# A three-layer cross-interaction tower: layer 0 from squares of pair sums, states spread over partitions by 0/1 matmuls, and a fully unrolled program

## What is computed

```python
e = stack([tbl_f[ids[:, f]] for f in range(32)], axis=1)      # (1024, 32, 16)
xk = x0 = e
for W in (W0, W1, W2):                                         # (32, 32, 64), (32, 64, 64), (32, 64, 64)
    xk = relu(einsum('bmd,bhd,mhk->bkd', x0, xk, W))
    outs.append(sum(xk, axis=2))
h = concatenate([concatenate(outs, axis=1), dense_ctx], axis=1)
h = maximum(h @ W_top1 + b_top1, 0); h = maximum(h @ W_top2 + b_top2, 0)
y = h @ W_top3
```

## Time and profile before

| what | value |
|---|---|
| runs | 786.91 us median of 3 (784.26 to 787.66) |
| profiled execution, first to last instruction (span) | 775.5 us |
| what the median has beside that span | 11.4 us |
| busy: TensorE, DVE, ACT, POOL | 593.1, 595.6, 408.5, 576.2 us |
| mean granted TensorE clock | 0.921 of full speed |

### The profile page before, as it was taken

How to read it: one execution, slowest core, us unless ns; L and a number is a source line. 1 busy time by engine, 2 the same in 40 slices (tenths; PEclk the granted TensorE clock), 3 DMA queues, 4 the chain that set the end, 5 groups by cost and what they waited for, 6 DMA issues and landing times.

```text
span 775.5 us, 8340 instructions
## 1 busy us (share of the span) xinstructions
PE 593.1 (76%) x2532; PEld 189.3 (24%) x2532; DVE 595.6 (77%) x325; ACT 408.5 (53%) x724; POOL 576.2 (74%) x340
## 2 busy tenths in 40 slices
PE   0256563998289978969499959769599959799998
PEld 0133111322023222213123212213132212222243
DVE  0143459999399969879799958799899969899910
ACT  0123480867238673746357745727367726657522
POOL 6775679698868889898868888898978887626400
PEclk9968795999779998989799999999899989999999
DMA  3799989794979789797979698897979697990000
GB/s 88 160 195 210 204 180 202 156 206 91 204 147 208 151 170 203 152 205 151 204 150 205 118 201 173 182 199 155 205 152 204 136 207 151 203 197 8 7 8 0
DMA packets 56099, 123.07 MB, mean 159 GB/s; under 512 B 16177, under 2 KB 25265, under 8 KB 56082
## 3 DMA queue, kind: packets, MB, share of 16 engines
q1 hardware_dynamic: 47890, 120.75, 76.8%
q0 software_dynamic: 8192, 2.11, 3.0%
HBM read 117.84 MB, written 4.20 MB: 157 GB/s over the span
## 4 chain that ended last, share of the span: by engine, by line
POOL 27%; DVE 18%; issue 16%; DMA 15%; PE 14%; ACT 5%; SPq 4%; POOLq 0%; DVEq 0%; ACTq 0%
DVE prod L455 16%; POOL gath L377 16%; POOL prod_pool L416 11%; PE acc L662 10%; DMA x<-x_scratch 8%; DMA gath<-in_tables,row_now 4%; ACT rep L568 4%; PE rep L769 2%; DMA x_scratch<-gath 2%; SPq L251 1%; DMA m_rep<-x_scratch 1%; DVE z_sb L471 1%; SPq L258 1%; SPq L255 1%; PE rep L760 1%
## 5 line engine op out<-in xcount | busy, mean ns | idle before, releaser
L662 PE MATMUL acc<-prod,w_sb 128*64 128x512 f32 x1728 | 425.2, 631 | 119.2 <-DVE prod L455 117.9
L455 DVE TENSOR_TENSOR prod<-m_rep,rep 128x2048 f32<-128x2048 f32 x186 | 416.1, 2273 | 17.9 <-DMA m_rep<-x_scratch 10.1
L377 POOL DMA_INDIRECT gath<-in_tables,row_now x256 | 287.1, 1121 | 81.8 <-issue 68.4
L416 POOL TENSOR_TENSOR prod_pool<-m_rep,xb_pool 128x2048 f32<-128x2048 f32 (+1 forms) x62 | 276.7, 4490 | 62.0 <-PE acc L662 54.6
L568 ACT ACTIVATE xb_pool<-acc 32x512 f32<-32x512 f32 x248 | 146.0, 589 | 162.4 <-PE acc L674 157.6
L662 PEld LDWEIGHTS acc<-prod,w_sb 128*64 128x64 f32 x1728 | 124.0, 144 | 407.4 <-issue 230.1
L568 ACT ACTIVATE rep<-acc 32x512 f32<-32x512 f32 x248 | 139.9, 564 | 68.4 <-DVE prod L455 63.4
L455 DVE TENSOR_TENSOR prod<-x_rot,x_rep 128x2048 f32<-128x2048 f32 x30 | 101.9, 3436 | 75.8 <-DMA x<-x_scratch 72.2
L662 PE MATMUL acc<-prod_pool,w_sb 128*64 128x512 f32 x496 | 117.2, 593 | 4.5 <-POOL prod_pool L416 4.5
L560 ACT ACTIVATE rep<-acc 64x512 f32<-64x512 f32 x124 | 70.7, 570 | 51.2 <-DVE prod L455 25.6
L704 PE MATMUL acc<-prod,w_sb 128*64 128x256 f32 x128 | 21.5, 498 | 48.5 <-DVE prod L508 48.4
(11 more groups left out here) (29 smaller groups left out, 90.3 us busy)
## 6 DMA issues: line engine op xcount, KB each, us to landing
m_rep<-x_scratch SPq DMA_DIRECT2D x56, 1024.0 KB, 23.3
x_rot<-x_scratch SPq DMA_DIRECT2D x60, 512.0 KB
x_rep<-x_scratch SPq DMA_DIRECT2D x60, 128.0 KB
m_rep<-x_scratch SPq DMA_DIRECT2D x12, 512.0 KB, 21.1
gath<-in_tables,row_now POOLq DMA_INDIRECT x256, 2.4
x_scratch<-gath SPq DMA_DIRECT2D x60, 64.0 KB
x<-x_scratch SPq DMA_DIRECT2D x30, 128.0 KB
x_rot<-x_scratch SPq DMA_DIRECT2D x8, 256.0 KB, 4.5
```

The costliest lines, as they stand in the source:

```text
L377: pool.indirect_dma_start(out=gath[par][:, g, :], out_offset=None, in_=tables, in_offset=bass.IndirectOffsetOnAxis(ap=row_now[par][:, g:g ...
L416: nc.gpsimd.tensor_tensor(prod_pool[:, u, :, 0:hi], m_tiles(p, T - 2 * POOL_UNITS + 2 * u, 2, 0, hi), xb_pool[l - 1][:, None, 0:hi].to_bro ...
L455: nc.vector.tensor_tensor(prod[:, slot, :, :], in0, in1[:, None, :].to_broadcast([128, 2, PAIR]), ALU.mult).then_inc(unit_ready, 1)
L662: last = nc.tensor.matmul(bank[K * a:K * a + K, :], w, chunk_of(p, tiles[i], a), start=start and i == 0, stop=stop and i == len(ws) - 1)
```

## The change

Layer 0 is computed otherwise. With x[m]x[h] = ((x[m]+x[h])^2 - x[m]^2 - x[h]^2)/2, TensorE forms the 496 sums of two rows in four tiles of 128 (`pair_sums`, a 0/1 matrix with 32 rows), ACT squares them from PSUM (`square`), TensorE multiplies the squares by (W0[m,h]+W0[h,m])/2 (`layer0`) and adds 32 squares of x0 with corrected weights (`layer0_diag`). `x_rep`, `x_rot`, `x16` and their loads go.

The states are spread by a 0/1 matmul (`replicate`): 32 rows of `state` to 128 partitions, two matmuls of 512 columns for each of `rep[0]` and `rep[1]`. This asks that the copies stand at partition 4h + q, so that a row's four copies are neighbours; ids, weights and limits are laid out so on the host. POOL takes its state from `xb`, one ACT copy of `rep[0]`.

The work is a list of 32 slots, (layer 1, pair p) and (layer 2, pair p - 1) in turn, all written out. From slot 3 on, DVE does 7 units a slot, the third of them 768 columns of each tile instead of 1024; POOL does the other 256 columns (`prod_edge`) and one whole unit. In slots 0 to 2 DVE does all 8. `x0_scratch` is stored once, in one DMA; `m_rep` is loaded by four DMAs of 1 MB with 8 KB runs. The layer-0 work of pair p + 1 stands between the units of slot (1, p), for slots 0 and 1 behind them. The first small weights are loaded by ACT's queue.

```diff
-            for p in range(first):
-                body(p, p % 2, p // 2)
-            with eng.Fori(first // 2, last // 2) as s:
+SLOTS = [(1, 0)]
+for _p in range(1, NP):
+    SLOTS += [(1, _p)] + ([(2, _p - 1)] if _p > 0 else [])
+SLOTS += [(2, NP - 1)]
...
@@ sync @@
+            for p in range(NP):
+                sp.wait_ge(gathered[p % 2], 16 * GPP * (p // 2 + 1))
+                sp.dma_start(flat, gath[p % 2][:, :, :].rearrange("r g d -> r (g d)")).then_inc(x0_stored, 16)
+                sp.wait_ge(x0_stored, 16 * (p + 1))
+                after(sp, l0_done, p - 1)
+                for a in range(2):
+                    sp.dma_start(x0c[p % 2][M * a:M * a + M, :],
+                                 x0_dram[p, :, CHUNK * a:CHUNK * a + CHUNK]).then_inc(x_in[p % 2], 16)
+                if p >= M_BUFS:
+                    last = SLOT_OF[(2, p - M_BUFS)]
+                    sp.wait_ge(unit_ready, UNIT_BASE[last + 1])
+                    after(sp, pool_ready, pool_before(last + 1))
+                for j in range(T // 2):
+                    sp.dma_start(m_tiles(p, 2 * j, 2), src).then_inc(m_first[j] if p == 0 else m_in[p % M_BUFS], 16)
...
@@ gpsimd @@
+            for p in range(4):
+                gather(p, 0, GPP)
+            for i in range(POOL_FROM, NS):
+                products(i)
+                p, half = 4 + (i - POOL_FROM) // 2, (i - POOL_FROM) % 2
+                if p < NP:
+                    gather(p, GPP // 2 * half, GPP // 2)
...
@@ vector @@
+                if pool_in(i):
+                    dve.wait_ge(xb_ready, i - POOL_FROM + 1)
...
+                for u in range(v0_units(i)):
+                    width = PAIR - EDGE if pool_in(i) and u == 2 else PAIR
+                    unit(base + u, m_tiles(p, 2 * u, 2, 0, width), rep[0], width)
+                dve.wait_ge(rep1_ready, i + 1)
+                for u in range(T // 2):
+                    unit(base + v0_units(i) + u, m_tiles(p, 2 * u, 2), rep[1])
...
@@ scalar @@
+            def square(p, t):
+                n = ST * p + t
+                act.wait_ge(sums_ready, n + 1)
+                after(act, sq_used, n - QB + 1)
+                nc.scalar.activation(sums_sq[:, n % QB, :], pair_sum[:, :], SQUARE).then_inc(sq_ready, 1)
+            def copy_rep0(i):
+                act.wait_ge(rep0_ready, i + 1)
+                after(act, pool_ready, pool_before(i - 1))
+                nc.scalar.copy(xb[i % 2][:, :], rep[0][:, :]).then_inc(xb_ready, 1)
+                if i > 0:
+                    act.wait_ge(unit_used, UNIT_BASE[i])
+                    relu_state(*SLOTS[i - 1])
+                if nxt is not None:
+                    square_x(nxt)
+                    square(nxt, 0)
+                    square(nxt, 1)
+                copy_rep0(i + 1)
+                if nxt is not None:
+                    square(nxt, 2)
+                    square(nxt, 3)
+                    relu0(nxt)
...
@@ tensor @@
+            def pair_sums(p, t):
+                n = ST * p + t
+                pe.wait_ge(x_in[p % 2], 32 * (p // 2 + 1))
+                after(pe, sq_ready, n)
+                for a in range(2):
+                    last = nc.tensor.matmul(pair_sum[:, CHUNK * a:CHUNK * a + CHUNK], sel_sb[M * a:M * a + M, t, :],
+                                            x0c[p % 2][M * a:M * a + M, :], start=True, stop=True)
+            def replicate(i, v):
+                for a in range(2):
+                    rows = slice(K * a + M * v, K * a + M * v + M)
+                    last = nc.tensor.matmul(rep[v][:, CHUNK * a:CHUNK * a + CHUNK], rsel_sb[rows, :],
+                                            state[l - 1][rows, :], start=True, stop=True)
+            for i, (l, p) in enumerate(SLOTS):
+                for u in range(nv):
+                    pe.wait_ge(unit_ready, base + u + 1)
+                    if u == nv - 1:
+                        if i > 0:
+                            replicate(i + 1, 0)
+                        if pool_in(i):
+                            pe.wait_ge(pool_ready, pool_before(i) + 1)
+                            edge = prod_edge[:, i % 2]
+                    unit(acc, base + u, [w[:, 0, 2 * u + k, :] for k in range(2)], u == 0, False, edge)
+                    if nxt is not None and u == 0:
+                        pair_sums(nxt, 0)
+                    if nxt is not None and u == 1:
+                        pair_sums(nxt, 1)
+                        layer0(nxt, 0)
+                if nxt is not None:
+                    pair_sums(nxt, 2)
+                    layer0(nxt, 1)
...
+                for u in range(T // 2):
+                    pe.wait_ge(unit_ready, number + 1)
+                    if final and i > 0:
+                        replicate(i + 1, 1)
+                    unit(acc, number, [w[:, 1, 2 * u + k, :] for k in range(2)], False, final)
+                    if nxt is not None and u == 0:
+                        pair_sums(nxt, 3)
+                        layer0(nxt, 2)
+                    if nxt is not None and u == 1:
+                        layer0(nxt, 3)
+                        layer0_diag(nxt)
```

More of the change, by code:

```diff
@@ L220, in in_chunk @@
-        def in_chunk(p, ap):
-            return ap.rearrange("p (h c) -> p h c", h=2) if isinstance(p, int) and p == 0 else ap
-        def pairs(eng, body, first, last):
-            for p in range(first):
-                body(p, p % 2, p // 2)
-            with eng.Fori(first // 2, last // 2) as s:
-                for par in range(2):
-                    body(2 * s + par, par, s)
-            for p in range(last, NP + 1):
-                body(p, p % 2, p // 2)
+            return m_rep[:, first:first + n, lo:hi]
@@ new lines, in unit @@
+            def unit(acc, number, ws, start, stop, edge=None):
+                src = prod[:, number % RING]
+                for k, w in enumerate(ws):
+                    first, final = start and k == 0, stop and k == len(ws) - 1
+                    last = nc.tensor.matmul(acc[0:K, :], w, src[:, k, 0:CHUNK], start=first, stop=final)
+                    if edge is None:
+                        last = nc.tensor.matmul(acc[K:2 * K, :], w, src[:, k, CHUNK:PAIR], start=first, stop=final)
+                    else:
+                        wide = CHUNK - EDGE
+                        nc.tensor.matmul(acc[K:2 * K, 0:wide], w, src[:, k, CHUNK:PAIR - EDGE], start=first, stop=final)
+                        last = nc.tensor.matmul(acc[K:2 * K, wide:CHUNK], w, edge[:, k, :], start=first, stop=final)
+                last.then_inc(unit_used, 1)
@@ L696, in _ @@
             pe.wait_ge(w0_ready, 1)
+            for t in range(ST):
+                last = nc.tensor.matmul(acc1[0:2 * M, 0:K], selt_sb[:, t, :], w0_sb[:, t, :], start=t == 0, stop=t == ST - 1)
+            last.then_inc(diag_summed, 1)
+            pair_sums(0, 0)
+            for t in range(1, ST):
+                pair_sums(0, t)
+                layer0(0, t - 1)
+            layer0(0, ST - 1)
+            pe.wait_ge(diag_ready, 1)
+            layer0_diag(0)
+            replicate(0, 0)
+            replicate(0, 1)
@@ L697, in _ @@
             pe.wait_ge(w1_in, 16)
             pe.wait_ge(w2_in, 16)
-            def add_half(bank, h, tiles, ws, start, stop):
-                for i, w in enumerate(ws):
-                    for a in range(2):
-                        last = nc.tensor.matmul(bank[K * a:K * a + K, HC * h:HC * h + HC], w,
-                                                tiles[:, i, HC * a:HC * a + HC],
-                                                start=start and i == 0, stop=stop and i == len(ws) - 1)
-                return last
```

693 lines of the change are left out of this document (223 added, 470 removed).

## The result

The changed kernel takes **809.24 us** (median of 4 runs, 804.99 to 811.29), the kernel before on the same chip 786.38 (784.26 to 787.66): ratio **1.0302, 95% interval 1.0257 to 1.0347**, thus 3% slower where 748 and faster were forecast. The profiled execution took 810.99 us with a span of 808.5. So 2.5 us lie outside this span, not the 11.4 that I added: the page of before, with its span of 775.5, must come from a faster execution (about 778 us) than those that make the median.

The account below looks back on a forecast made before the run. DVE and its chain were taken to bound the kernel before, TensorE the changed one. Start and slots 0 to 2 to 129, slots 3 to 31 to 704.5, perceptron 32.2: span 736.7, plus 11.4, 748 us against 786.9; range 728 to 815.

Parts of the forecast that it names:

- the 11.4: Time outside the profiled span: 11.4 us, added to the span of 736.7 to give 748.
- Start: Before DVE's first product: x0 store at 25.4, uncovered layer-0 chain of 12.5 us plus 4, DVE starting at 47.5.
- Slots 0 to 2: First three slots, with late layer 0 of pairs 1 and 2: end at 129 us, bounds 118 and 142.
- Slots 3 to 31: Steady part, TensorE-bound: 13 slots with layer 0 at 24.5 us, 16 without at 16.0, 574.5 in all, plus 1.
- island of 1.01 us: Each 32-row pair of matmuls (pair_sums, replicate, diagonal) on TensorE: 1.01 us, 0.15 over a pair in the stream.
- 0.34 us for both changes: Rejected pricing of form changes on TensorE: 0.17 us tail at each, 123 places, 23 us more, 771 in the end.
- DMA: Loads: 4 MB of m_rep a pair landing in 23.3 us, with over 32 us for it; costed at nothing.
- 1, serialised 32-row matmuls: TensorE runs the two 32-row matmuls one by one, 0.86 us more for each of 128: 850 us; chance 0.18.
- 2, the ring: pair_sums waiting for ACT's squares holds TensorE, then DVE: 30 to 50 us more, 790 us; chance 0.12.
- 3: DVE and TensorE couple less tightly, or loads and fetches come late: 1 us a slot, about 777; chance 0.14.
- 4: New matmuls nearly free, kernel stays DVE-bound: 645 us; chance 0.02, shared with a much shorter start.
- Late fetches: Instruction fetches of the unrolled program wait behind m_rep loads, up to 23 us each; chance 0.02.

Follow-up runs that it names:

- paced: Changed kernel with its first 64 gathers in four work-released runs of 16: 761.55 us, ratio 0.9878 (third chip); 785.36, 1.0007 (fourth); 786.53, 1.0021 (fifth).
- half-layer run: Changed kernel without the last two of four tiles of pair sums, squares and their matmuls for pairs 3 to 15 (wrong results): 708.02 us, third chip.
- run with the dummies: Changed kernel with 50 useless matmuls before the first pair_sums and four before each later step of the first layer 0: 833.63 us, first chip.
- the same stream: Kernel before with 100 useless matmuls ahead of TensorE's first work, beside gathers: 776.0 us on the third chip, 811.95 on the fourth, 812.22 or 812.10 on the fifth.

## Why the prediction was wrong, step by step

**The step that failed is *Start*: "a chain without cover ... 12.5 us ... DVE starts at 47.5".** The working of the chain was right: where gathers don't slow it (paced, third chip) DVE starts at 49.1. It left out that POOL's 64 gathers, which the change joins into one run up to 84 us, lie beside it; I had costed them by POOL's own time alone and called them free. In the kernel before only 32 run at first, from 4 to 46 us, and DVE's first layer-1 product begins at 44.16. What POOL costs others was not in my sum at all. What the runs showed in its place: beside the unbroken run a step of the chain takes 14 to 22 us instead of the 3.1 that I had. Cost: 97.7 - 47.5 = **50 us**; it turns 759 into 809.

**Slots 0 to 2**: 81.5 us forecast (47.5 to 129), measured 87.8 (97.7 to 185.5), and 87.8 in the paced kernel on the third chip as well. So these **6 us** belong to no stall. About half of them are the late layer 0 of slot 1, 15.3 us from relu to relu (153.1 to 168.4) where I had 12: from 157 on TensorE's granted clock is 0.56.

**Slots 3 to 31**: 575.5 forecast, 590.9 measured, **15 us**. The mis-sized term is the island of 1.01 us. TensorE's timeline around one, for the earlier trace rows:

```profile
395.72 0.59 PE L446 MATMUL acc<-prod,w_sb 128*64 128x512 f32 x1
...
396.25 1.13 PE L405 MATMUL pair_sum<-x0c,sel_sb 32*128 32x512 f32 x4
397.31 0.64 PE L446 MATMUL acc<-prod,w_sb 128*64 128x512 f32 x1
...
399.18 1.13 PE L405 MATMUL pair_sum<-x0c,sel_sb 32*128 32x512 f32 x4
400.23 1.08 PE L417 MATMUL acc<-sums_sq,w_sb 128*64 128x512 f32 x4
401.24 1.13 PE L438 MATMUL rep<-state,rsel_sb 32*128 32x512 f32 x4
402.30 0.64 PE L446 MATMUL acc<-prod,w_sb 128*64 128x512 f32 x1
```

The records of 395.72 take their 0.43 us of the stream, to 396.15, and the next begin at 397.31: an island takes 1.16 us, not 1.01, and the start behind it comes 0.48 us later instead of 0.43. Both changes of form together cost 1.16 - 0.86 + 0.05 = 0.35 us, not 0.15. Between two islands the square's matmul takes 1.01 where I had 0.86, so each change counts by itself. The earlier trace rows already had the longer island, and I read them short: 24 records from 420.00, at 1.72/8 each, end at 425.16 and not at 425.25, so that L674's island took 1.10 us there already. The 0.34 us for both changes, which I had worked out from the tail of 0.17 us and set aside, is what came. In the prediction it stood for 23 us more; the split matmul, for which I had 0.2 us in each of the 29 slots, cost nothing (6 us less), and that leaves 17 for the 15 measured.

The half-layer run prices a whole step at 4.1 / 2 = 2.05 us, against 0.86 + 1.01. Four steps at 0.2 more are 0.8 of the 1.2 us that a pair is longer; the four `replicate` and the diagonal add about 0.9, and the two splits take 0.4 off. The Trainium skill (TensorEngine Tiling (Array Packing), Key Properties) has a switch of tiling mode drain TensorE; the rows agree, with 0.35 us for the two switches around an island.

**The sum**: 736.7 + 50 + 6 + 15 = 808, the span. The tail was right (776.4 to 808.5 is 32.1). **The 11.4 us** beside the span are 2.5, so the time of this execution is off by 9 us less than its span. The baseline was too fast as well: a span of 775.5 belongs to a kernel of about 778, not 787. An estimate of what the change is worth without the stall is 775.5 - 758.5 = 17 us on that page, not 39; the paced kernel on the third chip measures 773.56 - 761.55 = 12.

**The parts off the path** held: squares 1.02 us (1.0), POOL 1.28 + 4.57 a slot (1.2 + 4.7), ACT 19%, DVE 459.3 us in the 29 slots with room to spare. *DMA*: costed at nothing, and right. The 23.3 us of the earlier trace rows was too high: the first 4 MB, from 30 us on, fill 14 slices of 0.75 us. DMA by slices, 30 to 60 us:

```profile
DMA  9999999999999941001010430577999899999999
GB/s 426 382 404 306 404 386 400 389 432 414 370 427 391 408 147 15 0 11 9 2 11 11 119 77 1 148 191 306 393 448 306 360 433 408 393 442 400 382 418 410
```

**The rivals.** *1, serialised 32-row matmuls*: fell; four records of `pair_sums` take 1.13 us together. *2, the ring*: near in time (790) but wrong in place: in slots 3 to 31 TensorE idles 1.6 us in all. What came true of it is that the ring has no cover in the start. *3*: the 15 us of form changes are half its size, and not its cause. *4*: fell. *Late fetches*: instruction packets rose from 8 to 24 and the slots show no hole. Nor do the traces' DMA records show a slow fetch in the slow stretch: in the changed kernel the only instruction packet from 0 to 110 us is one of 8 KB at 46.0 that took 0.3 us, and in the run with the dummies a packet of 16 KB had landed by 28.8 and the stretch went on for 60 us. Whether instructions are held up behind that can't be read from them. The range held 809 by luck, since its upper part stood for rival 2 and the cause was no rival of mine; the sign, at 0.69 for faster, did not hold.

**Open**: by what mechanism gathers slow TensorE, and ACT or the signals to it, on four of the five chips of the experiments and not on the third; how many in a row it takes (holes began 10 to 36 us into a run); what the changed kernel itself takes on the third chip (708.02 plus 13 x 4.1 makes an estimate of 761); and the 9 us of the kernel before, whose page with a span of 775.5 lies nearer to the third chip's spans (767.4 to 773.5) than to the others'.

## What to carry to other kernels

A chain of short steps between TensorE and ACT has to be costed beside what POOL issues at that time: a long run of indirect gathers stretched it here from 3.9 us a step to between 14 and 22, and breaking the run in blocks of eight, released by the work, got back about 33 us (1.030 against 0.988 of the kernel before, on different chips). Where matmul forms alternate, price each change from the end of the stream before it, not from the start of the first record behind it (0.35 us for the two around an island here, not 0.15), and group what has the same form. Set the profiled span against its own execution before a sum is built on what lies outside it.

## What was unexpected of the hardware

On the first, fourth and fifth chip of the experiments, independent matmuls on TensorE came mostly 0.7 to 3.5 us apart beside an unbroken run of gathers of 1.25 us each, and 0.24 us apart (29.42 us for 122) once these paused; on the second the chain of layer 0 was slow in the same way; on the third the same stream showed one spacing. The kernel before ran in 773.6 us on the third chip instead of 784 to 789, which the slow stretch doesn't explain, since its start is alike in the two traces with spans of 775.5 and 784.7. Two 32-row matmuls over all 128 columns do run side by side in float32, four records in 1.13 us. Four transfers of 1 MB with 8 KB runs landed in about 10.5 us.
